# Unused products, earlier gate products and earlier table loads in the small modules of a four-layer network

## The chip, the core and the metric

The kernel runs on one core of a Trainium2 chip, as one launch. The engines of the core work side by side, each through its own queue of instructions: TensorE (PE) multiplies matrices and turns them, VectorE (DVE) and ScalarE (ACT) work on elements, GpSimd (POOL) fills and converts, and SyncE (SP) issues most of the DMAs. They meet only in semaphores. The metric is the device time of one execution in microseconds; lower is better.

## The reference

A state x of 128 rows by 256 channels goes through four layers. Each layer adds three things to x in turn, each computed from a normalised x: a cross-attention over 12544 context rows, a small attention among the 128 rows themselves, and a feed-forward part. Cut to its lines:

```
x = x + _L0_xattn_ref(_layernorm(x, axis=-1), ctx_1024, ...)
x = x + _L0_attn_ref(...)      # one head, softmax over columns
x = x + _L0_ffn_ref(...)       # 16 experts, tokens chosen by each expert
x = x + _L1_xattn_ref(...)
x = x + _L1_attn_ref(...)      # delta rule with convolutions and a fusion gate
x = x + _L1_ffn_ref(...)       # 8 experts, two per token, layernorm and Gelu
x = x + _L2_xattn_ref(...)
x = x + _L2_attn_ref(...)      # one head
x = x + _L2_ffn_ref(...)       # fixed-point Gelu
x = x + _L3_xattn_ref(...)
x = x + _L3_attn_ref(...)      # windowed, rotary
x = x + _L3_ffn_ref(...)       # 8 experts, the nearest centroid's gate
```

All is in float32. The layernorm needs 1/sqrt(var + eps); the attentions need an exponential; L1_ffn needs the exact Gelu; L3_ffn a sigmoid.

## The kernel before

The twelve parts are twelve modules, named L0x, L0a, L0f (cross-attention, attention, feed-forward), then L1x to L3f. Each is a block with one hand-written queue for each engine, and all engines meet at the end of each block, so the order is that of the code. The four cross-attentions take 400 to 600 us each and loop over the context; the change touches none of their loops. The other eight modules take 12 to 74 us each. They are chains: one engine hands 128 rows to the next, and most engines wait most of the time.

A module begins with a layernorm (`norm_vector`, L1370, on VectorE; `norm_scalar`, L1381, the square root on ScalarE): statistics, variance plus eps, root, reciprocal, and the normalised tile. TensorE then turns the tile (`turn_chunks`, L1388), VectorE copies the result from PSUM to SBUF, and projections follow (`project_rows`, `project_turned`).

`keep_busy(e, bank, ident, n)` (L1360, the product at L1363) issues n products of the identity with itself into a PSUM bank whose content nobody reads. It stands in TensorE's queue where it would otherwise wait, and before the wait. The profile shows each such product as two matmuls and two weight loads, so n = 10 reads x20. It holds what is queued behind it until it is through.

ScalarE holds one table of functions at a time. The compiler puts an ACT_TABLE_LOAD ahead of the first activation that needs another table. In the modules before, the load for the layernorm's root stands at the start of the module.

Places that the change and the prediction touch:

- L1a (`delta_rule_attention`): TensorE turns the k rows (L1992), waits for the v rows and turns them (L1996), runs 10 unused products, then turns the normalised k rows and the kb rows (L1391). At its end it runs 18 unused products, turns o, and multiplies by wo.
- L1f (`top_two_experts`): 8 first-layer products of 128 x 512 (L1753), each added to its bias and measured on VectorE; after the fourth, VectorE picks two experts per token and makes `weight`. After the eighth, TensorE turns `weight` (L1757), VectorE copies it, TensorE multiplies it by b2 (L1760), and VectorE starts `acc` with it (L1840); then come the roots' reciprocal (L1842), the normalising (L1844), the turns, Gelu on ScalarE (L1799) and the second layer.
- L2f (`rounded_ffn`): the output bias is a product of one row (L2443) behind the last of the second-layer products (L2441).
- L3a (`window_attention`) and L3f (`nearest_expert`): L3a ends with a turn and the product by wo. L3f normalises x twice, scores the centroids (L3f_p_g), makes the input of each expert (L2768, with g and b that ScalarE's queue has loaded), and runs two first layers (L1399) before the first second layer (L1407). The turn of `weight` (L2720) and its product with b2 (L2723) stand between, and VectorE waits for both ahead of its half of the hidden rows (L2805).

## Time and profile before

| | us |
|---|---|
| median of 3 runs | 2319.34 |
| lowest, highest | 2318.71, 2323.18 |
| profiled execution | 2316.36 |
| its span | 2314.5 |
| mean granted clock in the span | 0.993 |
| PE, DVE, ACT, POOL busy | 2215.0, 1624.2, 1476.6, 414.0 |
| L1a, from its first VectorE instruction to that of L1f | 73.8 (1123.9 to 1197.7) |
| L1f, to that of L2x | 52.3 (1197.7 to 1250.0) |
| L3a, to that of L3f | 26.5 (2213.7 to 2240.2) |
| L3f, to the issue of the output's DMA | 71.6 (2240.2 to 2311.8) |

The span is what the profiler saw of the program; the execution took 1.9 us more than it. TensorE counts as busy for 96% of the span, but that holds the unused products and the pipelined ends of matmuls. The granted clock is a share of 2.4 GHz: 1.00 is 2.4 GHz, 0.50 is 1.2 GHz, and a value between is a stretch with both.

### The profile page before, as it was taken

To read this page: it belongs to the slowest core of one execution; us is meant where nothing else is said; L and a number is where in the kernel's file an instruction comes from. 1 tells how busy PE (TensorE), PEld (TensorE's weight loads), DVE (VectorE), ACT (ScalarE), POOL (GpSimd) and SP (SyncE) were. 2 spreads that over 40 slices of the span, in tenths; PEclk is the share of its full clock that TensorE was granted. 3 is DMA by queue.
4 is the path that set the end of the run, shared out by engine and by line. 5 is a ranking of instruction groups with operands and counts; after the bars stand their busy time and mean duration, and the time that the engine had idled before them with its cause. 6 is when DMAs were issued, how large, how long until landed. Compare 5 with 4: busy or idle time off the path is not lost. (4 is left out here: it accounts for less than half of the span.)

```text
span 2314.5 us, 75395 instructions
## 1 busy us (share of the span) xinstructions
PE 2215.0 (96%) x30367; PEld 1924.6 (83%) x30367; DVE 1624.2 (70%) x3699; ACT 1476.6 (64%) x3173; POOL 414.0 (18%) x356
## 2 busy tenths in 40 slices
PE   8999999988999999999899999999998999999989
PEld 7888888887888888888678888888887888888878
DVE  6787777536777777777664778777735877877732
ACT  3766776635878788878543677676642766667621
POOL 3222121003121212120002222222002212222000
PEclk9999999999999999999999999999999999999999
DMA  7777777375444444433512777777616777777471
GB/s 149 127 126 129 130 131 116 51 236 151 112 117 115 112 118 109 124 102 77 192 44 70 141 122 125 123 126 128 98 53 130 133 132 130 119 126 128 67 263 58
DMA packets 152487, 280.07 MB, mean 121 GB/s; under 512 B 32829, under 2 KB 72078, under 8 KB 152218
## 3 DMA queue, kind: packets, MB, share of 16 engines
q1 hardware_dynamic: 148842, 272.18, 57.2%
q10 hardware_dynamic: 3376, 4.03, 0.6%
q8 instruction: 203, 3.33, 0.6%
q14 instruction: 66, 0.54, 0.1%
HBM read 120.94 MB, written 0.33 MB: 52 GB/s over the span
## 5 line engine op out<-in xcount | busy, mean ns | idle before, releaser
L580 DVE CUSTOM_DVE_ANT_0 L1x_p_s<-L1x_p_s,L1x_mask,L1x_neg_max 128x512 f32<-128x512 f32 (+1 forms) x400 | 288.6, 742 | 56.5 <-PE L1x_p_s L339 54.3
L1259 DVE TENSOR_REDUCE L0x_tops<-L0x_m_bank 128x1 f32<-128x448 f32 x448 | 262.7, 618 | 83.0 <-PE L0x_m_bank L993 80.7
L1259 DVE TENSOR_REDUCE L3x_tops<-L3x_m_bank 128x1 f32<-128x448 f32 x448 | 262.4, 618 | 83.2 <-PE L3x_m_bank L993 80.9
L1259 DVE TENSOR_REDUCE L2x_tops<-L2x_m_bank 128x1 f32<-128x448 f32 x448 | 262.7, 619 | 79.7 <-PE L2x_m_bank L993 77.5
L473 ACT ACTIVATE L1x_prob<-L1x_p_s,L1x_neg_max 128x512 f32<-128x512 f32 (+1 forms) x400 | 274.5, 686 | 68.7 <-DVE L1x_neg_max L580 66.6
L1157 ACT ACTIVATE L0x_prob<-L0x_s_bank 128x512 f32<-128x512 f32 x448 | 220.4, 549 | 88.7 <-PE L0x_s_bank L1006 82.8
L1157 ACT ACTIVATE L3x_prob<-L3x_s_bank 128x512 f32<-128x512 f32 x448 | 220.4, 549 | 87.6 <-PE L3x_s_bank L1006 81.7
L1157 ACT ACTIVATE L2x_prob<-L2x_s_bank 128x512 f32<-128x512 f32 x448 | 220.4, 549 | 87.4 <-PE L2x_s_bank L1006 81.5
L348 PE MATMUL L1x_p_t<-net_ident,L1x_prob 128*128 128x128 f32 x1568 | 239.5, 274 | 13.6 <-ACT L1x_probT L189 11.4
L348 PEld LDWEIGHTS L1x_p_t<-net_ident,L1x_prob 128*128 128x128 f32 x1568 | 191.9, 141 | 56.7 <-ACT L1x_probT L189 23.5
L339 PE MATMUL L1x_p_s<-L1x_k_stack,L1x_q_stack 96*128 96x512 f32 (+1 forms) x400 | 181.7, 456 | 2.2 <-DVE L1x_q_stack L563 1.9
L189 ACT COPY L1x_probT<-L1x_p_t 128x512 f32<-128x512 f32 (+1 forms) x300 | 172.3, 575 | 1.8 <-PE L1x_p_t L348 1.6
L1006 PEld LDWEIGHTS L0x_s_bank<-L0x_q_sub,L0x_k_stack 52*128 52x128 f32 x1568 | 117.8, 187 | 24.8 <-issue 17.3
L1006 PEld LDWEIGHTS L3x_s_bank<-L3x_q_sub,L3x_k_stack 52*128 52x128 f32 x1568 | 117.5, 186 | 25.0 <-issue 17.4
L1006 PEld LDWEIGHTS L2x_s_bank<-L2x_q_sub,L2x_k_stack 50*128 50x128 f32 x1568 | 117.4, 186 | 24.8 <-issue 17.3
L1006 PE MATMUL L0x_s_bank<-L0x_q_sub,L0x_k_stack 52*128 52x128 f32 x1568 | 122.2, 266 | 3.0 <-ACT L0x_prob L1157 3.0
L1006 PE MATMUL L3x_s_bank<-L3x_q_sub,L3x_k_stack 52*128 52x128 f32 x1568 | 122.0, 266 | 3.0 <-ACT L3x_prob L1157 3.0
L1006 PE MATMUL L2x_s_bank<-L2x_q_sub,L2x_k_stack 50*128 50x128 f32 x1568 | 121.9, 265 | 2.8 <-ACT L2x_prob L1157 2.8
L364 PE MATMUL L1x_p_oT<-L1x_probT,L1x_v 128*32 128x128 f32 x3136 | 106.4, 276 | 0.5 <-ACT L1x_probT L189 0.5
L269 POOL CAST L1x_ctx_part<-L1x_ctx 128x1024 fp32r<-128x1024 f32 x24 | 25.4, 1058 | 409.7 <-DMA L1x_ctx<-in_ctxT 213.6
L1026 PE MATMUL L0x_s_bank<-L0x_prob,L0x_v 128*32 128x128 f32 x3136 | 97.2, 274 | 0.3 <-ACT L0x_prob L1157 0.3
L1026 PE MATMUL L3x_s_bank<-L3x_prob,L3x_v 128*32 128x128 f32 x3136 | 97.2, 274 | 0.3 <-ACT L3x_prob L1157 0.3
(821 smaller groups left out, 5589.4 us busy)
## 6 DMA issues: line engine op xcount, KB each, us to landing
L0x_k_stack<-L0x_kT SPq DMA_DIRECT2D x333, 112.0 KB, 4.0
L2x_k_stack<-L2x_kT SPq DMA_DIRECT2D x333, 112.0 KB, 4.0
...
```

The lines of the kernel that those rows point to most:

```text
L189: copy(probT[:, h % PT_RING, 0:nk], p_t[h % T_RING][:, 0:nk]).then_inc(sem(copied(h)), 1)
L269: e.tensor_copy(high, ctx[:, odd, :, 0:nk]).then_inc(sem("ctx_high"), 1)
L339: e.matmul(p_s[h % S_RING][:, 0:nk], q_stack[0:ROWS, h, :], k_stack[0:ROWS, odd, h // 2, 0:nk], start=True, stop=True).then_inc(sem("score ...
L348: i = e.transpose(p_t[h % T_RING][:, t * P:(t + 1) * P], prob[:, h % P_RING, t * P:(t + 1) * P], ident[:])
L364: i = e.matmul(p_oT[VW * s:VW * s + VW, g * P:(g + 1) * P], v[:, odd, t, h, :], probT[:, h % PT_RING, t * P:(t + 1) * P], start=t == 0, st ...
L473: e.activation(prob[:, h % P_RING, 0:nk], p_s[h % S_RING][:, 0:nk], ACT.Exp, bias=neg_max[:, odd, h:h + 1], scale=-1.0).then_inc(sem("expe ...
L580: e.tensor_tensor_reduce(s, s, mask[:, odd, 0:nk], -1.0, neg_max[:, 1 - odd, h:h + 1], ALU.add, ALU.min, neg_max[:, odd, h:h + 1]).then_in ...
L1006: mm = e.matmul(s_bank[s_at(u, r) % RING][:, at * P:(at + 1) * P], k_stack[rows_of(r), b % 2, slot_of(u), t * P:(t + 1) * P], q_sub[rows_o ...
L1026: mm = e.matmul(bank[32 * n:32 * n + VW, 2 * P:3 * P], v[:, b % 2, t, n // 2 * 8 + 2 * j + n % 2, :], prob[:, (2 * q + t // 4) % 3, n, t % ...
L1157: e.activation(prob[:, k % 3, u % 2 * 2 + r, 0:nt, :].rearrange("p t n -> p (t n)"), s_bank[n % RING][:, 0:nt * P], ACT.Exp).then_inc(sem( ...
L1259: e.tensor_reduce(tops[:, b % 2, h, half:half + 1], m_bank[n % RING][:, 0:HALF], AX, ALU.max).then_inc(sem("m_free"), 1)
```

## The change

Four kinds of edit, in the modules outside the cross-attentions' loops. A function `next_root` is new: an activation of one column with Sqrt, whose result nobody reads, put at the end of ScalarE's queue in all modules but L1a, L1f and L3f; the table is then loaded there. In L1f a Gelu of one column stands behind the roots. Unused products are added or taken away at 23 places in L1a, L1f, L2f, L3a and L3f. In L1f and L3f the turn of `weight`, its copy and its product with b2 stand earlier, and in L2f the bias product comes first.

```diff
@@ cross_attention, cross_attention_turned, one_head_attention, token_choice_experts, rounded_ffn, window_attention: end of the scalar queue
+            next_root(e, st)
...
+def next_root(e, st):
+
+    e.activation(st["warm"][:], st["ident"][:, 0:1], ACT.Sqrt)
...
@@ top_two_experts, tensor
-            keep_busy(e, p_y[1], ident, 10)
+            keep_busy(e, p_y[1], ident, 8)
             e.wait_ge(sem("ln_normed"), 1)
             turn_chunks(e, ident, p_x, xn).then_inc(sem("xn_turned"), 1)
-            keep_busy(e, p_y[1], ident, 6)
+            keep_busy(e, p_y[1], ident, 4)
             e.wait_ge(sem("xnT_copied"), 1)
             e.wait_ge(sem("gate_loaded"), 16)
             project_rows(e, p_g[:, 0:E], xnT, gate).then_inc(sem("gated"), 1)
-            keep_busy(e, p_y[1], ident, 3)
...
                 i.then_inc(sem("h_made"), 1)
-            e.wait_ge(sem("small_weights"), 80)
-            e.wait_ge(sem("weighted"), 1)
-            e.transpose(p_x[0:E, 0:P], weight[:], ident[:]).then_inc(sem("weight_turned"), 1)
-            keep_busy(e, p_y[1], ident, 12)
+                if x_ == 5:
+                    e.wait_ge(sem("small_weights"), 80)
+                    e.wait_ge(sem("weighted"), 1)
+                    e.transpose(p_x[0:E, 0:P], weight[:], ident[:]).then_inc(sem("weight_turned"), 1)
             e.wait_ge(sem("weightT_copied"), 1)
             e.matmul(p_g[:, 0:D], weightT[:], b2[:], start=True, stop=True).then_inc(sem("b2_made"), 1)
-            keep_busy(e, p_y[1], ident, 7)
+            keep_busy(e, p_y[1], ident, 13)
...
                 if x_ == 1:
-                    keep_busy(e, p_y[1], ident, 9)
+                    keep_busy(e, p_y[1], ident, 5)
@@ scalar
             e.activation(rstd[:, 0, :], rstd[:, 1, :], ACT.Sqrt).then_inc(sem("h_roots"), 1)
+            e.activation(st["warm"][:], ident[:, 0:1], ACT.Gelu)
@@ vector
+                if x_ == 5:
+                    e.wait_ge(sem("weight_turned"), 1)
+                    e.tensor_copy(weightT[:], p_x[0:E, 0:P]).then_inc(sem("weightT_copied"), 1)
...
-            e.wait_ge(sem("weight_turned"), 1)
-            e.tensor_copy(weightT[:], p_x[0:E, 0:P]).then_inc(sem("weightT_copied"), 1)
-            e.wait_ge(sem("b2_made"), 1)
-            link(e.tensor_tensor(acc[:], xn[:], p_g[:, 0:D], ALU.add))
...
+                if x_ == 1:
+                    e.wait_ge(sem("b2_made"), 1)
+                    e.tensor_tensor(acc[:], xn[:], p_g[:, 0:D], ALU.add).then_inc(sem("acc_begun"), 1)
@@ delta_rule_attention, tensor
             t.then_inc(sem("k_turned"), 1)
+            keep_busy(e, bank[7], ident, 14)
             e.wait_ge(sem("v_activated"), 1)
...
-            keep_busy(e, bank[6], ident, 18)
+            keep_busy(e, bank[6], ident, 28)
             e.wait_ge(sem("o_done"), 1)
             turn_chunks(e, ident, bank[1], flat(o)).then_inc(sem("o_turned"), 1)
+            keep_busy(e, bank[6], ident, 2)
             e.wait_ge(sem("oT_copied"), 1)
             project_rows(e, bank[2][:, 0:D], oT, wo).then_inc(sem("out_made"), 1)
+            keep_busy(e, bank[6], ident, 3)
@@ rounded_ffn, tensor
-            keep_busy(e, p_x, ident, 24)
+            keep_busy(e, p_x, ident, 22)
             e.wait_ge(sem("w2_loaded"), 32)
+            e.wait_ge(sem("steps"), 1)
+            e.matmul(p_o[:, 0:D], steps[:], b2[:], start=True, stop=False)
...
-            e.matmul(p_o[:, 0:D], steps[:], b2[:], start=False, stop=True).then_inc(sem("out_made"), 1)
+            i.then_inc(sem("out_made"), 1)
@@ window_attention, tensor
-            keep_busy(e, p_o, ident, 30)
+            keep_busy(e, p_o, ident, 33)
             e.wait_ge(sem("affine"), 1)
...
-            keep_busy(e, p_o, ident, 4)
+            keep_busy(e, p_o, ident, 10)
             e.wait_ge(sem("rotated"), 1)
...
+            keep_busy(e, p_o, ident, 3)
             e.wait_ge(sem("qkT_copied"), 1)
...
+            keep_busy(e, p_o, ident, 3)
             e.wait_ge(sem("probT_copied"), 1)
...
+            keep_busy(e, p_x, ident, 2)
             e.wait_ge(sem("o_done"), 1)
             turn_chunks(e, ident, p_t, o[:].rearrange("p h d -> p (h d)")).then_inc(sem("o_turned"), 1)
+            keep_busy(e, p_x, ident, 2)
             e.wait_ge(sem("oT_copied"), 1)
             project_rows(e, p_v[:, 0:D], oT, wo).then_inc(sem("out_made"), 1)
+            keep_busy(e, p_x, ident, 3)
@@ nearest_expert, tensor
-            keep_busy(e, p_y[1], ident, 10)
+            keep_busy(e, p_y[1], ident, 8)
             e.wait_ge(sem("ln_normed"), 1)
             turn_chunks(e, ident, p_x, xn).then_inc(sem("xn_turned"), 1)
+            keep_busy(e, p_y[1], ident, 2)
...
             project_rows(e, p_g[:, 0:E], xnT, cent).then_inc(sem("aff_made"), 1)
+            keep_busy(e, p_y[1], ident, 4)
             e.wait_ge(sem("ln2_normed"), 1)
             turn_chunks(e, ident, p_x, xh).then_inc(sem("xh_turned"), 1)
 
-            keep_busy(e, p_y[1], ident, 10)
+            keep_busy(e, p_y[1], ident, 5)
...
+                if n == 0:
+                    e.wait_ge(sem("weighted"), 1)
+                    e.transpose(p_x[0:E, 0:P], weight[:], ident[:]).then_inc(sem("weight_turned"), 1)
                 if n == 1:
                     e.wait_ge(sem("bias_loaded"), 32)
-                    e.wait_ge(sem("weighted"), 1)
-                    e.transpose(p_x[0:E, 0:P], weight[:], ident[:]).then_inc(sem("weight_turned"), 1)
-                    keep_busy(e, p_y[1], ident, 4)
                     e.wait_ge(sem("weightT_copied"), 1)
@@ vector
             e.tensor_tensor(weight[:], one[:], alpha[:], ALU.mult).then_inc(sem("weighted"), 1)
+            link(e.tensor_tensor(x[:], x[:], xn[:], ALU.add))
             e.wait_ge(sem("weight_turned"), 1)
             e.tensor_copy(weightT[:], p_x[0:E, 0:P]).then_inc(sem("weightT_copied"), 1)
-            link(e.tensor_tensor(x[:], x[:], xn[:], ALU.add))
-            e.wait_ge(sem("b2_made"), 1)
-            link(e.tensor_tensor(x[:], x[:], p_g[:, 0:D], ALU.add))
...
+                if x_ == 1:
+                    e.wait_ge(sem("b2_made"), 1)
+                    link(e.tensor_tensor(x[:], x[:], p_g[:, 0:D], ALU.add))
```

TensorE's queue in L1f, from the first-layer products (L1f_w is the experts' weights, net_ident the identity, x12 how often) to the first turns of the hidden rows, before:

```order
L1753 MATMUL L1f_p_h<-L1f_w,L1f_xnT 128x512 x16
L1757 MATMUL L1f_p_x<-net_ident,L1f_weight 8x128
L1363 MATMUL L1f_p_y<-net_ident 128x128 x12
L1760 MATMUL L1f_p_g<-L1f_b,L1f_weightT 128x256
L1363 MATMUL L1f_p_y<-net_ident 128x128 x7
L1391 MATMUL L1f_p_t<-net_ident,L1f_h 128x128 x8
L1363 MATMUL L1f_p_y<-net_ident 128x128 x9
```

and in the changed kernel:

```order
L1761 MATMUL L1f_p_h<-L1f_w,L1f_xnT 128x512 x12
L1766 MATMUL L1f_p_x<-net_ident,L1f_weight 8x128
L1761 MATMUL L1f_p_h<-L1f_w,L1f_xnT 128x512 x4
L1768 MATMUL L1f_p_g<-L1f_b,L1f_weightT 128x256
L1365 MATMUL L1f_p_y<-net_ident 128x128 x13
L1398 MATMUL L1f_p_t<-net_ident,L1f_h 128x128 x8
L1365 MATMUL L1f_p_y<-net_ident 128x128 x5
```

The turn of `weight` has moved ahead of the last two experts, the 12 unused products between it and the bias product are gone, and 7 have become 13.

VectorE's queue in L3f, from `weight` to the first expert's output, before:

```order
L2793 TENSOR_TENSOR L3f_weight<-L3f_one,L3f_alpha 128x8
L2795 COPY L3f_weightT<-L3f_p_x 8x128
L2796 TENSOR_TENSOR net_x<-net_x,L3f_xn 128x256
L2798 TENSOR_TENSOR net_x<-net_x,L3f_p_g 128x256
L2805 TENSOR_SCALAR L3f_h<-L3f_p_h,L3f_b 128x128 x4
L2768 TENSOR_SCALAR L3f_xe<-L3f_xhT,L3f_g,L3f_b 128x128 x2
```

and in the changed kernel:

```order
L2818 TENSOR_TENSOR L3f_weight<-L3f_one,L3f_alpha 128x8
L2819 TENSOR_TENSOR net_x<-net_x,L3f_xn 128x256
L2821 COPY L3f_weightT<-L3f_p_x 8x128
L2828 TENSOR_SCALAR L3f_h<-L3f_p_h,L3f_b 128x128 x4
L2793 TENSOR_SCALAR L3f_xe<-L3f_xhT,L3f_g,L3f_b 128x128 x2
L2828 TENSOR_SCALAR L3f_h<-L3f_p_h,L3f_b 128x128 x4
L2793 TENSOR_SCALAR L3f_xe<-L3f_xhT,L3f_g,L3f_b 128x128 x2
L2835 TENSOR_TENSOR net_x<-net_x,L3f_p_g 128x256
```

The addition of the bias product (L3f_p_g) has moved behind the hidden rows of the first two experts.

ScalarE's queue around L0a, before (a branch is the seam between two modules):

```order
L761 UNCONDITIONAL_BRANCH
L1480 UNCONDITIONAL_BRANCH
L1385 ACT_TABLE_LOAD
L1385 ACTIVATE L0a_ln_rstd<-L0a_ln_rstd 128x1
L1487 ACTIVATE L0a_kT<-L0a_p_k,L0a_bk 128x128 x2
L1494 ACT_TABLE_LOAD
L1494 ACTIVATE L0a_prob,L0a_total<-L0a_s,L0a_low 128x128
L1440 UNCONDITIONAL_BRANCH
```

and in the changed kernel:

```order
L1370 ACT_TABLE_LOAD
L1370 ACTIVATE net_warm<-net_ident 128x1
L762 UNCONDITIONAL_BRANCH
L1487 UNCONDITIONAL_BRANCH
L1392 ACTIVATE L0a_ln_rstd<-L0a_ln_rstd 128x1
L1494 ACTIVATE L0a_kT<-L0a_p_k,L0a_bk 128x128 x2
L1501 ACT_TABLE_LOAD
L1501 ACTIVATE L0a_prob,L0a_total<-L0a_s,L0a_low 128x128
L1370 ACT_TABLE_LOAD
L1370 ACTIVATE net_warm<-net_ident 128x1
L1447 UNCONDITIONAL_BRANCH
```

The load stands ahead of the seam, and none stands ahead of the module's own root. The same holds at nine seams (into L0a, L0f, L1x, L1a, L2a, L2f, L3x, L3a and L3f).

## Rows read from the trace of the kernel before

**Rows 1.** Windows: length, busy us (count) of PE, PEld, DVE, ACT, POOL, clock, DMA, GB/s.
```profile
1134.00:1137.40 3.40, 0.01 (x1) 0.00 (x0) 3.04 (x11) 3.26 (x9) 0.00 (x0) 1.00 1.03 368
...
1195.90:1202.90 7.00, 6.24 (x28) 5.53 (x27) 1.86 (x7) 0.66 (x2) 0.60 (x16) 0.51 0.40 126
```

**Rows 2.** Timeline, the start of L0a and its end.
```profile
464.52 1.28 ACT L1385 ACT_TABLE_LOAD   x1 [3.91 <-PEq L761]
464.52 2.31 PEld L1363 LDWEIGHTS L0a_p_o<-net_ident 128*128 128x128 f32 x20 [0.46 <-issue]
...
465.23 0.15 DVE L1375 TENSOR_SCALAR L0a_ln_rstd<-L0a_ln_mean_var 128x1 f32<-128x1 f32 x1
...
466.75 0.25 PEld L1391 LDWEIGHTS L0a_p_x<-net_ident,L0a_xn 128*128 128x128 f32 x2
...
475.01 0.19 ACT L1494 ACTIVATION_READ_ACCUMULATOR L0a_prob<-L0a_s,L0a_low 128x1 f32 x1
...
476.50 0.42 DVE L1527 TENSOR_TENSOR net_x<-net_x,L0a_p_o 128x256 f32<-128x256 f32 x1 [0.79 <-PE L0a_p_o L1478]
```

**Rows 3.** Timeline, L1a, TensorE and VectorE; columns: start, duration, engine, line, operation.
```profile
1137.57 3.94 PEld L1363 LDWEIGHTS L1a_bank<-net_ident 128*128 128x128 f32 x20
...
1138.06 0.42 DVE L2239 TENSOR_TENSOR L1a_kb<-L1a_nat,L1a_beta 128x256 f32<-128x256 f32 x1
```

**Rows 4.** Timeline from the end of L1a into L1f.
```profile
1187.76 4.10 PEld L1363 LDWEIGHTS L1a_bank<-net_ident 128*128 128x128 f32 x36
...
1193.99 0.42 DVE L2360 TENSOR_TENSOR L1a_o<-L1a_o,L1a_onorm 128x256 f32<-128x256 f32 x1
...
1195.42 1.54 PE L1407 MATMUL L1a_bank<-L1a_wo,L1a_oT 128*128 128x256 f32 x4 [0.52 <-DVE L1a_oT L2362]
...
1197.69 4.34 PEld L1363 LDWEIGHTS L1f_p_y<-net_ident 128*128 128x128 f32 x20 [1.45 <-issue]
...
1199.02 0.41 DVE L1378 TENSOR_SCALAR L1f_xn<-net_x,L1f_ln_mean_var,L1f_ln_rstd 128x256 f32<-128x256 f32 x1
1201.91 0.44 PEld L1391 LDWEIGHTS L1f_p_x<-net_ident,L1f_xn 128*128 128x128 f32 x2
...
1205.04 0.30 PEld L1753 LDWEIGHTS L1f_p_h<-L1f_w,L1f_xnT 128*128 128x128 f32 x2
```

**Rows 5.** Timeline, the end of L3a and the first third of L3f.
```profile
2237.30 2.08 PE L1407 MATMUL L3a_p_v<-L3a_wo,L3a_oT 128*128 128x256 f32 x4 [0.52 <-DVE L3a_oT L2624]
...
2240.17 4.07 PEld L1363 LDWEIGHTS L3f_p_y<-net_ident 128*128 128x128 f32 x20 [1.52 <-issue]
...
2241.52 0.44 ACTq L2738 DMA_DIRECT2D L3f_b<-in_L_ffn_ln_b  x1
...
2246.95 3.94 PEld L1363 LDWEIGHTS L3f_p_y<-net_ident 128*128 128x128 f32 x20
...
2247.72 1.12 DVE L2768 TENSOR_SCALAR L3f_xe<-L3f_xhT,L3f_g,L3f_b 128x128 f32<-128x128 f32 x4
...
2250.82 7.23 PEld L1399 LDWEIGHTS L3f_p_h<-L3f_xe,L3f_w 128*128 128x128 f32 x64
...
2261.66 0.51 PEld L1407 LDWEIGHTS L3f_p_y<-L3f_w,L3f_h 128*128 128x128 f32 x3 [2.21 <-issue]
```

**Rows 6.** Timeline of L1f behind its last first-layer product.
```profile
1222.31 0.21 ACT L1792 ACTIVATE L1f_rstd<-L1f_rstd 128x8 f32<-128x8 f32 x1 [13.54 <-DVE L1f_rstd L1836]
...
1223.32 0.42 DVE L1840 TENSOR_TENSOR L1f_acc<-L1f_xn,L1f_p_g 128x256 f32<-128x256 f32 x1 [0.86 <-PE L1f_p_g L1760]
...
1224.77 0.91 PEld L1391 LDWEIGHTS L1f_p_t<-net_ident,L1f_h 128*128 128x128 f32 x8
...
1225.56 1.28 ACT L1799 ACT_TABLE_LOAD   x1 [3.04 <-PE L1f_p_t L1391]
```

**Rows 7.** Timeline, the end of L2f.
```profile
1746.02 0.69 PE L2443 MATMUL L2f_p_o<-L2f_b,L2f_steps 1*128 1x256 f32 x2
```

**Rows 8.** Tile L3f_b: time from issue to landing of its DMAs.
```profile
DMA to landing us min/median/max: 6.0/6.0/6.0
```

More of the change, by code:

```diff
@@ L1211, in _ @@
                     rise(g // WAVES - 1)
+            next_root(e, st)
         @block.vector
@@ L1494, in _ @@
             e.activation(prob[:], s[:], ACT.Exp, bias=low[:, 0:1], accum_out=total[:]).then_inc(sem("exped"), 1)
+            next_root(e, st)
         @block.vector
@@ L1637, in _ @@
                              bias=b12[:, 1, x_:x_ + 1]).then_inc(sem("h2_done"), 1)
+            next_root(e, st)
         @block.vector
@@ L1845, in _ @@
                                 ALU.subtract, ALU.mult).then_inc(sem("h_normed"), 1)
+                if x_ == 1:
+                    e.wait_ge(sem("b2_made"), 1)
+                    e.tensor_tensor(acc[:], xn[:], p_g[:, 0:D], ALU.add).then_inc(sem("acc_begun"), 1)
+            e.wait_ge(sem("acc_begun"), 1)
             for x_ in range(E):
@@ L2440, in _ @@
                 for fc in range(half * 4, half * 4 + 4):
-                    e.matmul(p_o[:, 0:D], hT[:, fc, :], w2[:, fc, :], start=fc == 0, stop=False)
-            e.wait_ge(sem("steps"), 1)
-            e.matmul(p_o[:, 0:D], steps[:], b2[:], start=False, stop=True).then_inc(sem("out_made"), 1)
+                    i = e.matmul(p_o[:, 0:D], hT[:, fc, :], w2[:, fc, :], start=False, stop=fc == FC - 1)
+            i.then_inc(sem("out_made"), 1)
         @block.scalar
@@ L2469, in _ @@
             ends(1)
+            next_root(e, st)
         @block.vector
@@ L2585, in _ @@
                              accum_out=total[:, h:h + 1]).then_inc(sem("exped"), 1)
+            next_root(e, st)
         @block.vector
@@ L2819, in build @@
     m = Module(nc, "net")
-    st = {n: m.sb(n, shape) for n, shape in (("x", [P, D]), ("ident", [P, P]), ("stack_rows", [P, 2]))}
+    st = {n: m.sb(n, shape) for n, shape in (("x", [P, D]), ("ident", [P, P]), ("stack_rows", [P, 2]), ("warm", [P, 1]))}
     with nc.Block() as block:
```

## The prediction

> **What bounds the kernel now.** The page first: TensorE is busy for 96% of the span, but in the eight small modules much of that is unused products, so the share says nothing there. The table under "Time and profile before" gives their lengths; L1a, L1f, L3a and L3f, in which nearly all edits lie, take 224 us together. What a change there is worth must be read link by link in the timeline.
>
> The windows view comes second, for the granted clock. TensorE stood still from 1134.0 to 1137.4, and ran the whole stretch from 1195.9 to 1202.9 at 0.51, which is the 1.2 GHz level for nearly all of it [rows 1]. The level is also seen in the unused products: 10 of them, x20 in a row, take 2.31 us in L0a [rows 2], but 3.94 in L1a [rows 3], 4.34 at the start of L1f [rows 4], 4.07 and 3.94 in L3f [rows 5]. Each slow stretch follows one in which TensorE did little.
>
> Third, the timeline around those products, for what stood behind them. In L1a the last input of the next turn is ready at 1138.48 (1138.06 + 0.42), and the unused products ahead of the turn run until 1141.51 [rows 3]. In L1f the normalised x is ready at 1199.43, and its turn starts at 1201.91 [rows 4]. So at half clock the unused products themselves are the path.
>
> **The change, term by term.** At full clock two passes of an unused product take 0.223 us of the queue: in L0a the turn starts 2.23 us after the first of 10 products [rows 2]. All terms are made against the profiled execution's own 2316.36 us.
>
> Term 1, the middle of L1a. The 14 new products fill 3.1 us of the 3.4 us in which TensorE waits for the v rows [rows 1]; they end before 1137.2 and cost nothing (at half clock they would cost 2.7 us). If the clock then stays up, the next 10 take 2.31 instead of 3.94 [rows 2, 3]: -1.6. The kb rows are ready a microsecond before that. Bounds: 0 if the clock falls anyway, -1.6.
>
> Term 2, the end of L1a. 28 products from 1187.76 take 28 x 0.223 = 6.2 us and end at 1194.0; o is ready at 1194.41 (1193.99 + 0.42), so they fit with 0.4 us to spare [rows 4]. The product by wo then takes about 1.04 us in place of 1.54 [rows 4]: the same product at half clock took 2.08 [rows 5], and full clock halves that. But three unused products now follow it, 0.67 us, against VectorE's last addition of 0.42 us beside them; the block ends with the later of them. I take 0.3 of the 0.5 as given back: -0.2 (bounds 0 and -0.5).
>
> Term 3, the head of L1f. Before, from 1197.69 to the first expert's product at 1205.04: 7.35 us [rows 4]. After: 8 products are through at +1.8, and x is normalised at +1.74 (1199.43 less 1197.69 [rows 4]), so the turn starts at +1.8. The copy of its result (0.42) and the steps around it end at about +2.9; 4 products behind the turn are through at +2.95. The gate product takes 0.45, and no unused products follow: the first expert's product starts at +3.45. That is -3.9. Bounds: -1.4 if the clock is low (8 x 0.434 = 3.5 in place of 4.3, 5 others fewer), -4.2. The expert biases come by DMA on ScalarE's queue at the same distance from the start as before, and could hold the first addition by up to a microsecond.
>
> Term 4, the tail of L1f. Before, the roots are done at 1222.52, but VectorE then waits for the bias product and adds it until 1223.74; only then come the reciprocal, the normalising, the turn at 1224.77, a table load of 1.28 from 1225.56 and the Gelu at 1226.84 [rows 6]. After: the reciprocal follows the roots at once, the turn starts at about 1223.35, and the Gelu table has been loaded since 1223.8; the 13 products end at 1222.9. Gelu starts at about 1224.15: -2.7. The copy of `weight` (0.27) and the addition to `acc` (0.42) now stand among other work of VectorE, which has over a microsecond of slack at both places. Bounds: -1.3 (the load alone) and -2.7.
>
> Term 5, the end of L2f: the bias product of 0.69 us at 1746.02 goes from the path [rows 7]: -0.6 (bounds -0.3 and -0.7).
>
> Term 6, L3a. It waits for weights at its head, so 33 products for 30 cost nothing; the others (0.45 to 1.3 us) fit into waits of TensorE. What remains is the product by wo, 2.08 us at half clock [rows 5]: 1.05 less, of which the trailing products give back 0.25: -0.8 (bounds 0 and -1.05).
>
> Term 7, L3f. Before, from 2240.17 to the first second layer at 2261.66: 21.5 us [rows 5]. Two waits would go: the unused products at half clock and the bias product ahead of VectorE's hidden rows. But a third is right behind them. The experts' g and b are loaded by ScalarE's queue; b was issued at 2241.52 and landed 6.0 us later, at 2247.5, and the experts' inputs were started at 2247.72 [rows 5, 8]: 7.4 us after the module's start, for b as for VectorE. The issue hangs on the variance and not on the table, so it stays at +1.35, and b lands at +7.35 though the rest is ready at about +4.9. Hence: inputs of the first expert at +8.0, two first layers of 7.23 together [rows 5] until +15.3, turn and bias product 0.6, second layer at +15.9. That is -5.6. Bounds: -3.0 if only the reordering counts, and -7.6 if b lands early.
>
> Term 8, the tables. A load of 1.28 us stands ahead of each root [rows 2], and in L0a the variance is ready at 465.38, 0.42 us before the load ends at 465.80 [rows 2]. Moving it makes x ready 0.4 us earlier at nine places. But the turn there starts at 466.75, exactly 2.23 us after the 10 unused products did [rows 2]: TensorE's own products hold it, whenever x is ready. They stay 10 or more in L0a, L0f, L1x, L1a, L2a, L2f, L3x and L3a, so nothing is gained; only L3f has 8, and is counted in term 7. The moved loads cost nothing where ScalarE has time: in L0a, the tightest, its last instruction ends at 475.20, load and root by 476.7, VectorE at 476.92 [rows 2]. Term: 0 (bounds +1 and -3.8, nine times 0.42).
>
> The Trainium skill ("ScalarE: Activation LUTs", What ACT_TABLE_LOAD costs) speaks against this: it adds a drain of about 1.38 us to each switch. By that rule load and root would end at 478.1 in L0a, 1.2 us behind VectorE, and the sum would be some 3 us smaller over the tight seams; the trace does not agree, since in L0a the loads before cost no more than their 1.28 us: the turn, which stands behind the root, three steps of VectorE and 1.28 us of load, started at 2.23 us, and with a drain it could not have.
>
> Sum: -1.6 -0.2 -3.9 -2.7 -0.6 -0.8 -5.6 = -15.4. 2316.36 - 15.4 = 2301.0 for a profiled execution; the median of the runs lies 3.0 above it, so the median after should be near 2303.9.
>
> **Rivals.** (a) The clock falls elsewhere or stays low at one of the four places, since new idle times lie differently. For it speaks that L3f still has TensorE waiting 1 to 2 us for b; against it, that the waits of TensorE between L0a's few rows went without one: its unused products took 2.31 us, full clock [rows 2]. It takes terms 1 to 3 (5.7) or much of 6 and 7 (about 4): about 2309. The Trainium skill ("TensorE: Matmul & The Clock Gate", Part 1) says that the activity window is free-running, so the same kernel counts different numbers of slow matmuls from run to run; if so, part of what the trace shows as lost is luck of that execution, and 2309 would be the time. One profile cannot show that.
>
> (b) The table loads do pay, because the products' hold on the turn is softer than it looks, or b lands earlier: up to 3.8 and 2.0 more; in the middle, some 5 us, about 2299.
>
> (c) Slower. The added products run at half clock and become the path: 0.434 us each. At 1187.76 they would end at 1199.9 in place of 1194.0, 5.5 us after o is ready; the 14 cost 2.7, and 33 in L3a 14.3 us, against 7.3 at full clock: some 7 us behind the weights. Terms 4, 5 and the reordering of L3f give back 6.3. Put together: 5.5 + 2.7 + 7 - 6.3 = 8.9, about 2328. It decides as soon as the 28 take more than 6.65 us, 0.238 us each. Against it: before, 18 in the same place took 4.10 us, full clock [rows 4].
>
> (d) The change doesn't do what it says: the compiler puts a load ahead of the roots again. The rows of ScalarE's queue show none, so for the tables this is out; it would cost 9 x 0.2 us and leave about 2306.
>
> **Chances.** Forecast 0.68, (a) 0.16, (b) 0.10, (c) 0.03, (d) 0.03. What this measurement can tell from no change is about 0.2%, 4.6 us. The forecast, (b) and (d) are all faster by more; of (a) and its worse mixtures I leave 0.04 within 4.6 us, and 0.02 to mixtures of (c). Faster 0.92, same 0.04, slower 0.04. Range: 2298 to 2310.
>
> **What would show it.** In the changed profile: clock 1.00 from 1134 through L1f's head and from L3a's end into L3f; x20 behind the v turn in 2.3 us; from L1f's start to its first expert's product 3.5 us; no table load between L1f's first hidden turns and Gelu; from L3f's start to the first second layer 15.9 us, with TensorE waiting for VectorE's L3f_xe; L0a, L0f and L2a as long as before. A module's end set by ScalarE's table load, or an x20 of over 3 us, would prove me wrong.

## The result and the profile after

| | before | after |
|---|---|---|
| median of the runs, us | 2319.34 (5 runs: the three above and two more) | 2303.03 (5 runs) |
| lowest, highest | 2316.30, 2323.18 | 2300.38, 2305.28 |
| profiled execution, us | 2316.36 | 2303.03 |
| its span, mean clock | 2314.5, 0.993 | 2301.2, 0.996 |

The changed kernel takes 0.9925 of the time of the kernel before (95% interval 0.9909 to 0.9940), 16.3 us less by the medians; 2303.9 was forecast. The profiled execution, however, was forecast at 2301.0 and took 2303.03: only the median came out, see below. The share of busy time tells nothing here either: TensorE is at 96% in both.

```profile
PE 2214.2 (96%) x30421; PEld 1923.9 (84%) x30421; DVE 1624.9 (71%) x3699; ACT 1479.2 (64%) x3183; POOL 412.9 (18%) x356
```

The lengths of the modules tell it. Each is the distance between two modules' first VectorE instructions (of L3f to the span's end, good to 0.05 us). The columns e1 and e9 are two further executions of the same changed kernel (e1 and e9 below).

| us | before | after | e1 | e9 | forecast change |
|---|---|---|---|---|---|
| L0x | 464.55 | 469.44 | 481.48 | 466.78 | 0 |
| L0a | 12.67 | 12.57 | 12.47 | 12.54 | 0 |
| L0f | 53.24 | 53.11 | 53.18 | 53.38 | 0 |
| L1x | 593.45 | 591.66 | 593.66 | 591.88 | 0 |
| L1a | 73.81 | 73.42 | 71.64 | 71.72 | -1.8 |
| L1f | 52.30 | 45.59 | 45.58 | 45.59 | -6.6 |
| L2x | 460.60 | 461.60 | 461.59 | 460.49 | 0 |
| L2a | 12.76 | 12.70 | 12.79 | 12.84 | 0 |
| L2f | 24.56 | 24.65 | 24.68 | 24.09 | -0.6 |
| L3x | 465.78 | 461.43 | 466.42 | 466.38 | 0 |
| L3a | 26.48 | 26.69 | 26.72 | 28.30 | -0.8 |
| L3f | 74.30 | 68.34 | 68.29 | 68.21 | -5.6 |

The small modules together went down by 13.05 us in the profiled execution. The cross-attentions, whose loops were not edited, moved by +4.9, -1.8, +1.0 and -4.35, which happens to add up to -0.25. One span against another would mislead: e1 is the same program, and its span is 2318.5.

The clock first, in the stretches that answer to [rows 1], and at the end of L1a (columns: length, busy of PE, PEld, DVE, ACT, POOL, clock, DMA, GB/s):

```profile
1136.90:1140.30 3.40, 3.31 (x30) 3.11 (x28) 3.08 (x10) 3.25 (x9) 0.00 (x0) 1.00 0.99 349
1189.20:1197.10 7.90, 7.90 (x58) 7.90 (x58) 5.19 (x17) 2.75 (x4) 0.00 (x0) 0.78 0.00 0
1198.50:1205.80 7.30, 7.00 (x46) 5.57 (x45) 2.85 (x11) 0.98 (x2) 0.59 (x16) 1.00 0.45 128
2232.80:2239.60 6.80, 5.60 (x46) 5.28 (x46) 3.43 (x12) 1.69 (x3) 0.60 (x16) 1.00 1.02 326
```

The first stretch is the one in which TensorE stood still before; now it is busy for 3.3 of the 3.4 us. The heads of L1f and L3f (third and fourth) run at 1.00, where before L1f's had 0.51 and L3f's was at half clock (1.2 GHz) for its first 3.7 us. But the second stretch is at 0.78: half clock has come up at a place that had full clock before. The timeline of L1a shows both (columns: start, duration, engine, line, operation):

```profile
1136.81 3.21 PEld L1365 LDWEIGHTS L1a_bank<-net_ident 128*128 128x128 f32 x28
...
1140.65 2.31 PEld L1365 LDWEIGHTS L1a_bank<-net_ident 128*128 128x128 f32 x20
```
and before, the v turn and the turn behind the 10 products:
```profile
1137.40 0.20 PEld L1996 LDWEIGHTS L1a_bank<-net_ident,L1a_act 128*128 128x128 f32 x2 [3.63 <-DVE L1a_act L2233]
...
1141.43 0.25 PEld L1391 LDWEIGHTS L1a_bank<-net_ident,L1a_nat 128*128 128x128 f32 x2
```
The end of L1a and the head of L1f, after:
```profile
1189.22 7.96 PEld L1365 LDWEIGHTS L1a_bank<-net_ident 128*128 128x128 f32 x56
...
1195.45 0.43 DVE L2375 TENSOR_TENSOR L1a_o<-L1a_o,L1a_onorm 128x256 f32<-128x256 f32 x1
1197.10 0.25 PEld L1398 LDWEIGHTS L1a_bank<-net_ident,L1a_o 128*128 128x128 f32 x2
...
1200.17 1.86 PEld L1365 LDWEIGHTS L1f_p_y<-net_ident 128*128 128x128 f32 x16 [0.46 <-issue]
...
1201.97 0.24 PEld L1398 LDWEIGHTS L1f_p_x<-net_ident,L1f_xn 128*128 128x128 f32 x2
...
1203.51 0.30 PEld L1761 LDWEIGHTS L1f_p_h<-L1f_w,L1f_xnT 128*128 128x128 f32 x2
```

The 14 new products take 3.21 us ahead of the v turn, and the 10 behind it 2.31 in place of 3.94 [rows 3]; from the v turn to the next turn it is 2.40 us (1140.48 to 1142.88) in place of 4.03. At the end of L1a, 28 products take 7.96 us in place of the 6.2 expected. o is ready at 1195.88 (1195.45 + 0.43), and the turn starts at 1197.10: TensorE's own products hold it for 1.2 us. Then L1f: its first expert's product comes 3.34 us after the start, 7.35 before [rows 4].

The tail of L1f, to lay beside [rows 6]:

```profile
1220.78 0.21 ACT L1800 ACTIVATE L1f_rstd<-L1f_rstd 128x8 f32<-128x8 f32 x1 [11.16 <-DVE L1f_rstd L1848]
1221.01 1.28 ACT L1801 ACT_TABLE_LOAD   x1
...
1221.86 0.87 PEld L1398 LDWEIGHTS L1f_p_t<-net_ident,L1f_h 128*128 128x128 f32 x8
...
1222.62 1.51 ACT L1808 ACTIVATE L1f_a<-L1f_p_t,L1f_b1n,L1f_g 128x128 f32<-128x128 f32 x4
```

From the roots to Gelu it takes 1.84 us (1220.78 to 1222.62), before 4.54 (1222.31 to 1226.85). The table load starts behind the root and lies beside VectorE's first normalised rows and the turn; ScalarE starts Gelu 0.33 us behind it.

L3f, to lay beside [rows 5]:

```profile
2232.83 1.86 PEld L1365 LDWEIGHTS L3f_p_y<-net_ident 128*128 128x128 f32 x16 [0.46 <-issue]
...
2234.18 0.44 ACTq L2763 DMA_DIRECT2D L3f_b<-in_L_ffn_ln_b  x1
...
2238.25 0.42 DVE L2787 COPY L3f_xhT<-L3f_p_x 128x256 f32<-128x256 f32 x1 [1.07 <-PE L3f_p_x L1398]
...
2239.64 1.11 DVE L2793 TENSOR_SCALAR L3f_xe<-L3f_xhT,L3f_g,L3f_b 128x128 f32<-128x128 f32 x4 [0.97 <-DMA L3f_b<-in_L_ffn_ln_b]
...
2247.81 0.69 PE L2748 MATMUL L3f_p_g<-L3f_b,L3f_weightT 8*128 8x256 f32 x2
...
2248.43 0.73 PEld L1414 LDWEIGHTS L3f_p_y<-L3f_w,L3f_h 128*128 128x128 f32 x4 [0.33 <-issue]
```

VectorE stands still for 0.97 us until b has landed, and starts the experts' inputs 6.8 us after the module's start; the second layer follows at +15.6 in place of 21.5. And the seams, in L0a and L2f:

```profile
470.31 0.20 ACT L1392 ACTIVATE L0a_ln_rstd<-L0a_ln_rstd 128x1 f32<-128x1 f32 x1 [3.30 <-DVE L0a_ln_rstd L1382]
...
471.64 0.25 PEld L1398 LDWEIGHTS L0a_p_x<-net_ident,L0a_xn 128*128 128x128 f32 x2
...
475.11 1.13 PE L1406 MATMUL L0a_p_q<-L0a_xnT,L0a_wq 128*128 128x128 f32 x8 [1.64 <-DMA L0a_bv<-in_L_attn_bv]
...
480.00 1.28 ACT L1370 ACT_TABLE_LOAD   x1
...
481.29 0.42 DVE L1535 TENSOR_TENSOR net_x<-net_x,L0a_p_o 128x256 f32<-128x256 f32 x1 [0.79 <-PE L0a_p_o L1485]
```
```profile
1725.26 3.81 PE L2447 MATMUL L2f_p_h<-L2f_xnT,L2f_w 128*128 128x128 f32 x32 [1.37 <-DMA L2f_w<-in_L_ffn_w]
```

In L0a the root starts with no load before it, 0.87 us after the module's start in place of 1.26. The turn still comes at +2.23, and behind it the q product waits for bv's DMA until +5.7. The load at the end (480.00 to 481.28) lies under VectorE's last steps.

### The profile page after: what moved, and what is told of

It is laid out like the page before. It is cut to its first block and busy times, and to the rows that moved or that the text cites. A ratio compares the mean times of both kernels' runs of the same rounds, so it can differ in the third digit from the quotient of the medians.

```text
span 2301.2 us, 75514 instructions
## 1 busy us (share of the span) xinstructions
PE 2214.2 (96%) x30421; PEld 1923.9 (84%) x30421; DVE 1624.9 (71%) x3699; ACT 1479.2 (64%) x3183; POOL 412.9 (18%) x356
## 3 DMA queue, kind: packets, MB, share of 16 engines
q10 hardware_dynamic: 3376, 4.03, 0.6%
## 6 DMA issues: line engine op xcount, KB each, us to landing
L3f_w<-in_L_ffn_w SPq DMA_DIRECT2D x16, 1024.0 KB, 12.1
```

## The experiments

All were profiled, so that each module is compared with its own length in the tables. The timed ratios stand beside them, each with its 95% interval, against the kernel before on the same chip: e1 to e4 on one chip, e5 to e8 on a second, e9 to e11 on a third.

**e1 and e9: the changed kernel again, twice.** No edit.

> The changed kernel, unaltered, in another execution. Theory 1 (the gain lies in L1f and L3f and is fixed by the code): L1f is 45.6 us again and L3f 68.3, each within 0.2; L0x, which read 469.4 in the first profile and 464.6 in that of the kernel before though its loop was not edited, lies anywhere between 463 and 471, as do L3x (461 to 467) and L2x. Whether TensorE falls to half clock behind the fusion gate of L1a (28 products in 7.96 us) is luck of the execution: L1a is 73.4 with it and 72.2 without. Rival (the longer L0x belongs to the change, by the table load at its end or by code that lies elsewhere): L0x is 469 to 470 again, and L1a 73.4 again.

> The changed kernel once more, beside the version with all three further edits, on one chip. Theory 1: L1f 45.6 and L3f 68.3 within 0.2 for the third time; L1a 71.6 if TensorE keeps the clock behind the fusion gate, 73 to 75 if not; no half clock at the heads of L1f and L3f nor at L1a's v turn. Ratio to the kernel before 0.993. Rival (the places of half clock are free): it shows at one of these three places.

Measured: in e1 0.9932 of the kernel before (0.9913 to 0.9951), in e9 0.9934 (0.9905 to 0.9963). L1f is 45.58 and 45.59, L3f 68.29 and 68.21. L0x reads 481.5 and 466.8: its length belongs to the execution, not to the change, and 481.5 is well outside the range that I had given. L1a is 71.64 and 71.72, without half clock:

```profile
1202.68 6.33 PEld L1365 LDWEIGHTS L1a_bank<-net_ident 128*128 128x128 f32 x56
...
1209.38 0.20 PEld L1398 LDWEIGHTS L1a_bank<-net_ident,L1a_o 128*128 128x128 f32 x2 [0.37 <-DVE L1a_o L2375]
```

The 28 products take 6.33 us there and the turn waits for o (0.37 us idle) and not for them. The expected 72.2 was too high by 0.6; 0.35 of it is the head, where the v turn came 13.14 us after the start, 13.49 before. L3a in e9 took 28.30: TensorE was at half clock from 2215.8 to 2219.2.

**e2: the table edits alone**, on the kernel before.

```diff
+            next_root(e, st)                                   (nine scalar queues)
+            e.activation(st["warm"][:], ident[:, 0:1], ACT.Gelu)   (L1f)
```

> The kernel before with only the ten table edits: the root's table loaded at nine seams, and Gelu's behind the roots of L1f. Theory 1 (TensorE's 10 unused products and the weights' DMAs hold each head, not the root): L0a, L0f, L1a, L2a, L2f and L3a as long as before within 0.15 us, save for the landing of their weights; L1f shorter by 1.3 (Gelu's load), L3f by 0 to 0.1; in all -1.3, ratio 0.9994. Rival (the root is on the path at each seam): 0.4 less in each of nine modules, in all -5.1, ratio 0.9978.

Measured: 0.9989 (0.9970 to 1.0008). L0a, L0f and L2a are within 0.11 us of before. The interval holds both the 0.9994 of theory 1 and the 0.9978 of the rival; the lengths decide between them. L1a, L2f and L3a, which I had expected within 0.15 as well, are 0.73, 0.23 and 0.34 shorter; in L1a and L3a 0.40 and 0.42 of it lie from the product by wo to the end, where half clock stood before. L1f is 49.10, 3.2 less. From the roots to Gelu it takes 3.26 us, before 4.54: 1.28 less. But the second layer follows Gelu after 2.08 us (1221.21 to 1223.29), before after 1.56 (1226.85 to 1228.41), because the 9 unused products in between now hold it; in the changed kernel they are 5, and it is 1.55. The second layer in the kernel before:

```profile
1228.41 1.59 PEld L1407 LDWEIGHTS L1f_p_y<-L1f_w,L1f_a 128*128 128x128 f32 x8 [0.68 <-ACT L1f_a L1799]
```

The head is 2.45 less, and that is clock, without any edit that could steer it:

```profile
1195.78 2.31 PEld L1365 LDWEIGHTS L1f_p_y<-net_ident 128*128 128x128 f32 x20 [1.13 <-issue]
...
1200.68 0.30 PEld L1762 LDWEIGHTS L1f_p_h<-L1f_w,L1f_xnT 128*128 128x128 f32 x2
```
```profile
1217.95 0.21 ACT L1801 ACTIVATE L1f_rstd<-L1f_rstd 128x8 f32<-128x8 f32 x1 [12.83 <-DVE L1f_rstd L1846]
...
1221.21 1.15 ACT L1809 ACTIVATE L1f_a<-L1f_p_t,L1f_b1n,L1f_g 128x128 f32<-128x128 f32 x3 [1.54 <-PE L1f_p_t L1398]
...
1223.29 0.74 PEld L1414 LDWEIGHTS L1f_p_y<-L1f_w,L1f_a 128*128 128x128 f32 x4
```

The same 10 products, 4.34 us before, take 2.31 here, and the head takes 4.90 us with all its 19 products. So of the 4.0 us that L1f's head gained in the changed kernel, 2.45 (7.35 to 4.90) are clock and 1.56 (4.90 to 3.34) are fewer products. One small module went the other way: L3f took 76.4, with half clock in its head and again at its first second layer.

**e3: the moved instructions alone**, on the kernel before: the turn of `weight`, its copy and its product with b2 in L1f and L3f, and L2f's bias product first.

> The kernel before with only the moved instructions: in L1f and L3f the turn of weight, its copy and its product with b2, with the 12, 7 and 4 unused products beside them made 13 and 0, and in L2f the bias product first. Theory 1 (terms are separate waits): L1f -1.4 of its 52.3, L2f -0.6 (its weights' landing aside), L3f -3.0 of its 74.3, in all about -5, ratio 0.9978. Rival (the order is worth nothing while TensorE is at half clock around it, or it is worth all of the gain): L1f and L3f unchanged within 0.3, or L3f -6.

Measured: 0.9970 (0.9953 to 0.9986). L1f's tail from the roots to Gelu is 3.11 us, 1.43 less; its head was slower by 0.3, so L1f is 51.19 (-1.1, where -1.4 was expected). L2f is 0.45 shorter. L1a, which has no edit here, took 74.95, with 6.8 us of half clock around its v turn. L3f is 70.51, 3.8 less where 3.0 was expected: in this execution the 10 products behind the second turn ran at full clock (2.31 us for 3.94 before).

```profile
2246.34 2.31 PEld L1363 LDWEIGHTS L3f_p_y<-net_ident 128*128 128x128 f32 x20
...
2256.65 0.51 PEld L1407 LDWEIGHTS L3f_p_y<-L3f_w,L3f_h 128*128 128x128 f32 x3 [0.33 <-issue]
```

**e4: the numbers of unused products alone**, on the kernel before, at every place that the moves do not touch.

> The kernel before with only the numbers of unused products changed, at every place of the change that the moves do not touch. Theory 1: the clock is up in L1a's middle and at the heads of L1f and L3f, so L1f -3.9 (48.4), L3f -2.6 (71.7, b's landing holds the rest), L1a -0.4 to -1.8, L3a -0.8 from its first turn to its end; in all about -8, ratio 0.9965. Rival (the clock is luck, and the products do not steer it): half clock shows again at one of the heads of L1f and L3f in this execution, and its module gains less than 2.

Measured: 0.9983 (0.9966 to 1.0000), less than the 0.9965 expected. L1a is 71.94 (-1.9) and L1f 48.29 (-4.0). In L3f the first second layer starts at +18.7 in place of 21.5 (-2.8), as forecast; but TensorE fell to half clock just there, and L3f in all gained only 1.1:

```profile
2267.29 5.00 PEld L1407 LDWEIGHTS L3f_p_y<-L3f_w,L3f_h 128*128 128x128 f32 x16 [2.21 <-issue]
```

The 16 weight loads take 5.00 us; in the changed kernel's trace they take 3.32. Neither theory had half clock at that place. What stands ahead of it is the wait of 2.2 us that e3's moves take away. Of the four traces that have this wait, three show half clock right there (e2, e4 and e11, not before); of the nine without it, none. So the moves save more than their own wait.

The three parts took 0.0011, 0.0030 and 0.0017 off the time, 0.0058 together, where the whole took 0.0068 in e1 on the same chip. That agrees within the intervals, which are 0.002 to each side; the timed runs alone could not price the parts more finely.

**e11: the 14 products alone**, on the kernel before.

```diff
             t.then_inc(sem("k_turned"), 1)
+            keep_busy(e, bank[7], ident, 14)
             e.wait_ge(sem("v_activated"), 1)
```

> The kernel before with only the 14 unused products ahead of the v turn in L1a. Theory 1 (TensorE's wait of 3.6 us there makes the clock fall): no half clock at the 10 products behind the v turn, which take 2.3 us in place of 3.9; the heads of L1f and L3f, with nothing changed before them, show half clock again at one of them at least. L1a about 72.2, L1f 50 to 52.5. Rival (the clock at L1a's turn is luck): x20 behind the v turn takes 3 to 4 us in this execution too.

```profile
1137.60 0.20 PEld L1997 LDWEIGHTS L1a_bank<-net_ident,L1a_act 128*128 128x128 f32 x2 [0.46 <-DVE L1a_act L2234]
...
1137.77 2.31 PEld L1363 LDWEIGHTS L1a_bank<-net_ident 128*128 128x128 f32 x20
...
1140.00 0.25 PEld L1391 LDWEIGHTS L1a_bank<-net_ident,L1a_nat 128*128 128x128 f32 x2
```
The heads of L3f and L1f, in the columns of the clock table above:
```profile
2244.00:2257.30 13.30, 12.11 (x56) 11.64 (x57) 5.54 (x23) 3.18 (x5) 0.60 (x16) 0.51 0.92 308
1195.00:1200.00 5.00, 4.24 (x25) 4.14 (x25) 1.76 (x6) 0.20 (x1) 0.59 (x16) 0.66 0.37 121
```

Measured, one execution: 2.31 us behind the v turn, 2.40 from that turn to the next, before 4.03. That is the 1.63 expected. L1a is 71.46, 2.35 less, but the other 0.72 lies elsewhere: the v turn came 0.32 earlier in the module, and from the product by wo to the end it took 1.89 us in place of 2.29, at full clock where the trace of before has half. The heads that were left as before have half clock again: 0.66 in L1f's, and in L3f a whole stretch of 13.3 us at 0.51, which makes L3f 77.62.

**e5: 8 products for 10 at five heads**, on the changed kernel.

```diff
-            keep_busy(e, ..., ident, 10)
+            keep_busy(e, ..., ident, 8)
             e.wait_ge(sem("ln_normed"), 1)
```

> The changed kernel with 8 unused products in place of 10 ahead of the first turn of L0a, L0f, L1a, L2a and L2f, so that the earlier root can start the turn at +1.8 us in place of +2.23. Theory 1 (behind the turn the head waits for DMAs: bv in L0a, the biases in L0f, the mask in L2a, w1 in L2f, Wv in L1a): the first turn moves by 0.45 at each, and the modules keep their lengths within 0.15 us, L1a at most 0.4 shorter; ratio to the changed kernel 1.000. Rival (the two products hid the gain of the table loads): each of the five is 0.4 shorter, 2.1 in all.

```profile
465.79 1.86 PEld L1365 LDWEIGHTS L0a_p_o<-net_ident 128*128 128x128 f32 x16 [0.46 <-issue]
...
471.54 0.63 PEld L1406 LDWEIGHTS L0a_p_q<-L0a_xnT,L0a_wq 128*128 128x128 f32 x5 [2.34 <-issue]
```

Measured: 0.9961 (0.9938 to 0.9983). The turn comes at +1.79, and the q product at +5.75 as ever, for bv. L0a is 12.67, L0f 53.32, L2a 12.94, L2f 24.31 (12.57, 53.11, 12.70 and 24.65 before this edit). So the two products hid nothing. L1a, expected at most 0.4 shorter, rose to 76.59: Wv's DMA made TensorE wait 1.33 us at its head, half clock followed, and at its end it was at half clock for 6.8 us, where the 28 products took 8.98. e8 and e10 have the same 8 products at that head, and L1a at 72.29 and 71.78, so the 76.59 belong to this execution.

**e6: L3f's small loads early**, on the changed kernel.

```diff
@@ window_attention, scalar
             norm_scalar(e, m, "ln2", scratch2)
+            load_small(e)            (the DMAs of L3f's cent, g and b)
@@ nearest_expert
-            e.dma_start(cent[:], chunked(w["cent"])).then_inc(sem("cent_loaded"), 16)
-            e.dma_start(g[:], w["g"]).then_inc(sem("affine_loaded"), 16)
-            e.dma_start(b[:], w["b"]).then_inc(sem("affine_loaded"), 16)
```

> The changed kernel with the DMAs of L3f's cent, g and b issued by ScalarE's queue in L3a, behind its two roots, in place of in L3f. Theory 1 (b's landing at +6.8 holds the experts' inputs, and cent's the second turn): the inputs start at +5.3 to +5.9 from the module's start in place of +6.78, L3f is 0.9 to 1.5 us shorter than 68.3, and VectorE no longer waits for L3f_b. Rival (the weights of the first expert or TensorE's products are right behind): L3f within 0.3 of 68.3.

```profile
2237.98 0.42 DVE L2791 COPY L3f_xhT<-L3f_p_x 128x256 f32<-128x256 f32 x1 [0.53 <-PE L3f_p_x L1398]
2238.44 1.11 DVE L2797 TENSOR_SCALAR L3f_xe<-L3f_xhT,L3f_g,L3f_b 128x128 f32<-128x128 f32 x4
```

Measured: 0.9960 (0.9933 to 0.9988). The experts' inputs start at +5.3 (2238.44 less 2233.13) and directly behind the copy; L3f is 66.87, 1.4 less. b's landing was the bound, as the third wait of term 7 says: 0.97 us. The rest is cent, which had held the gate product for 0.87 us; without it the copy ahead of the inputs starts at +4.85 in place of +5.39. The timed ratios of e5 and e6 (0.996 both) lie above the 0.993 that the changed kernel had on two other chips. On this chip it was not timed, so what these two edits do to the whole time is not shown; the lengths show what they do to their modules.

**e7: a semaphore for each group of weights** in L0a, L2a and L3a, and 22 unused products for 28 at the end of L1a, on the changed kernel.

```diff
-            e.wait_ge(sem("weights"), 16 * len(loads))
+            e.wait_ge(sem("wq_loaded"), 16)
             project_turned(e, p_q, wq, xnT)
+            e.wait_ge(sem("wk_loaded"), 16)
@@ window_attention, vector (and so on for wqkv, cos and sin, mask, wo)
-            e.wait_ge(sem("weights"), 16 * len(loads))
+            e.wait_ge(sem("ln_loaded"), 32)
@@ delta_rule_attention, tensor
-            keep_busy(e, bank[6], ident, 28)
+            keep_busy(e, bank[6], ident, 22)
```

> The changed kernel with one semaphore for each group of weights in L0a, L2a and L3a in place of one for all, so that each product waits for its own weights, in the order of their use (8 and 4 unused products at the head of L0a and L2a, 18 for 33 in L3a), and 22 unused products for 28 at the end of L1a. Theory 1 (the last of the small DMAs holds these heads): the query product starts at about +3.5 in place of +5.6 in L0a and +5.0 in L2a; L0a 11.0 (from 12.6), L2a 11.5 (12.7), L3a 24 (26.7), and L1a 71.6 whether or not TensorE is at half clock behind the fusion gate. Rival (DMAs of one queue land together, so a semaphore of one's own brings nothing, or idle TensorE falls to half clock): these three within 0.4 of before, or shorter heads with half clock in the rows behind.

```profile
1184.76 6.62 PEld L1365 LDWEIGHTS L1a_bank<-net_ident 128*128 128x128 f32 x44
...
1191.46 0.20 PEld L1398 LDWEIGHTS L1a_bank<-net_ident,L1a_o 128*128 128x128 f32 x2
```
```profile
2226.88 0.42 SPq L2719 DMA_DIRECT2D L3f_cent<-in_L_ffn_centroids  x1
...
2234.82 0.99 PE L1414 MATMUL L3f_p_g<-L3f_cent,L3f_xnT 128*128 128x8 f32 x4 [5.19 <-DMA L3f_cent<-in_L_ffn_centroids]
```

Measured: 0.9941 (0.9916 to 0.9967). L0a is 10.58, L2a 10.67, L3a 22.70, 2 to 4 us less each. In L1a TensorE was at half clock behind the fusion gate for 3.4 us; the 22 products ended at 1191.38, o was ready at 1191.41 and the turn started at 1191.46: 72.01, not 73.4. But L3f rose to 74.16. L3a is 4 us shorter, the DMAs of the experts' weights issued in it are not, and cent, issued behind them on SyncE's queue, landed 7.8 us after its issue. The last weights issued ahead of it had landed at +7.59, and cent at +7.75; in the changed kernel these are +3.26 and +3.42, in the kernel before +3.41 and +3.57. TensorE stood still for 5 us, and half clock followed (the 4 products behind the gate product took 1.83 us, where the same row in the changed kernel has 0.97). That was in neither theory.

**e8 and e10: all three edits together**, on the changed kernel.

> The edits of the last three together, on the changed kernel. Theory 1: the three terms add up, some 6 us less than the changed kernel: about 0.9905 of the kernel before. Rival (what is saved at a head is lost to half clock or to the experts' weights behind it): not below 0.992.

> The version with all three further edits once more. Theory 1: L0a 10.3, L3a 23.0, L3f 67.0 within 0.3 each, and 6 us less than the changed kernel on the same chip: ratio to the kernel before about 0.990. Rival (its last measurement was a lucky one): the ratio is that of the changed kernel within 0.001.

Two rows of e10:

```profile
466.93 0.23 PEld L1398 LDWEIGHTS L0a_p_x<-net_ident,L0a_xn 128*128 128x128 f32 x2
...
468.04 0.97 PEld L1406 LDWEIGHTS L0a_p_q<-L0a_xnT,L0a_wq 128*128 128x128 f32 x8
```
```profile
2232.07 1.11 DVE L2810 TENSOR_SCALAR L3f_xe<-L3f_xhT,L3f_g,L3f_b 128x128 f32<-128x128 f32 x4
```

Measured: e8 0.9918 (0.9885 to 0.9951); e10 0.9881 (0.9853 to 0.9909). e8 alone cannot tell its theory (0.9905) from its rival (not below 0.992); e10 can. It ran on the chip on which the changed kernel had 0.9934 (e9): medians of 2295.60, 2307.53 and 2322.41 us. L0a is 10.26 and 10.37, L3a 22.96 and 22.46, L3f 66.96 and 66.95: with cent loaded early, the shorter L3a costs L3f nothing. L2a is 10.77 in e10 but 12.38 in e8, where its own first weight landed late (TensorE waits 1.6 us for wq). This version beats both kernels: the changed kernel by 7.7 us in e8 and 9.7 in e10 by the lengths of L0a, L2a, L3a and L3f, and by 11.9 in e10 by the medians on one chip; about 6 was expected.

## Why the prediction was right, term by term

The sum was -15.4 and the medians say -16.3; on the chips of e1 and e9 they say -16.3 and -14.9. That the forecast number came out so closely is in part luck. The profiled execution is only 13.3 us shorter, 2.1 less than the sum: 1.2 by the clock at L1a's end, 0.7 and 1.0 by weights that landed later at the heads of L2f and L3a, less some 0.8 of small gains elsewhere. The forecast then put the median 3.0 above the profiled execution, as it had been before, and this time it was 0.0 above. The two misses nearly cancel. The mechanisms stand on the terms:

- Term 1 (L1a's middle, -1.6): as forecast. From the v turn to the next turn 4.03 us became 2.40, -1.63, in the changed kernel and in e11, which has this edit alone. No half clock was seen behind the v turn in any of the ten traces that have the 14 products, and it was in all three that lack them (before, e2, e3).
- Term 2 (L1a's end, -0.2): wrong in the profiled execution: the turn of o starts 1.23 us behind o, before 0.05. The product by wo and what follows it give back 0.2, as forecast (2.29 us became 2.09). The step that failed is "28 x 0.223 = 6.2 us": it takes full clock there for granted, because the 18 products had it in the one trace of before. What stands ahead is unchanged, yet half clock shows there in the first trace of the changed kernel, e2, e5, e6, e7 and e8, and not in before, e1, e3, e4, e9, e10 and e11. This was rival (c)'s mechanism, at one place and at 7.96 us against the 12.1 (28 x 0.434) that it had counted. Its sign, 28 products over 6.65 us, was given; its price of 5.5 us was not, since only 3.4 us there were at half clock, and its other two places, the 14 and the 33, stayed at full clock. In e1 and e9 the term is as forecast.
- Term 3 (L1f's head, -3.9): measured -4.0. The reason needs an addition: e2 had full clock there without the edit. So 1.56 us (seven products fewer) are certain, and 2.45 are gained only over executions like that of before. The bound of -1.4 for a low clock does not follow from the prediction's own prices: seven products fewer at 0.434 us are 3.0.
- Term 4 (L1f's tail, -2.7): measured -2.70; from e3 1.43 for the order, from e2 1.28 for Gelu's load. The prediction counted up to Gelu only; e2 shows that 0.5 of the load's share would have been lost behind it without the cut from 9 unused products to 5.
- Term 5 (L2f, -0.6): from the second layers' start to the end, 10.14 us became 9.57, -0.57; e3 has L2f 0.45 shorter. In the profiled execution the module's length hides it (24.65), since its w1 landed 1.6 us later at the head.
- Term 6 (L3a, -0.8): from the first turn on, 18.83 us became 18.02. The head again hides it: the mask's DMA took 4.8 us in place of 3.8.

```profile
DMA to landing us min/median/max: 3.8/3.8/3.8
```
```profile
DMA to landing us min/median/max: 4.8/4.8/4.8
```

- Term 7 (L3f, -5.6): measured -5.9 (the second layer at +15.6 for +21.5), with b landed at +6.7, not +7.35 (5.4 us from its issue, 6.0 before). e3 and e4 give 3.8 and 2.8 to the second layer's start, e6 shows that b was next.
- Term 8 (tables, 0): right. Nine loads moved, and no module but L1f and L3f is shorter for it. But the named reason was only the first of two: the unused products hold the turn, and e5 shows that without them a DMA does. The drain that the Trainium skill ("ScalarE: Activation LUTs", What ACT_TABLE_LOAD costs) adds to each switch is not in these traces: in L1f the load began at 1221.01, took 1.28 us, and the next activation started at 1222.30. In this trace 19 of the 31 loads have the next activation 0.01 us behind them.

Whether the clock is steered or luck can be counted over all 13 traces:

| half clock | with the waits of before | with the change's products or order |
|---|---|---|
| behind L1a's v turn | 3 of 3 | 0 of 10 |
| at L1f's head | 3 of 4 | 0 of 9 |
| from L3a's end into L3f's head | 4 of 4 | 0 of 9 |
| at L3f's first second layer | 3 of 4 | 0 of 9 |
| behind L1a's fusion gate (nothing ahead of it changed) | 1 of 4 | 5 of 9 |

So filling or removing a wait of TensorE does keep the clock up at the place behind it. Behind the fusion gate, where nothing was done, it comes and goes with the execution; 1 of 4 and 5 of 9 are too few to say that the change plays no part there. (In e5 and e7 half clock also showed in L3f at +6.3 and +6.7, behind a longer wait for cent.)

Of the rivals, (a) is partly true without having decided: half clock did come up elsewhere. The page of the Trainium skill ("TensorE: Matmul & The Clock Gate", Part 1) by which the same kernel counts slow matmuls differently from run to run is borne out: the three traces of the changed kernel have half clock at different places, L1a's end in one of three. (b) and (d) fell: e5 found nothing hidden, of b's 2.0 us only 0.6 came, and no load stands ahead of a moved root. I had put (a) at 2309; in effect it cost the profiled execution 1.2 us at L1a's end (of the 1.8 between 73.42 and e1's 71.64, the other 0.6 is the head, where the v turn came at +13.70 for +13.14), and the cross-attentions' -0.25 cost nothing.

What stays open: why L0x took 481 us in e1 and L3x 476 in e4. L0x had 17.1 us at half clock in e1 and 3.4 in before, L3x 13.6 in e4 and 3.4 in before. Some 10 to 14 us more at half speed lose 5 to 7 at most, of the 17 and 10.5 that these modules were longer; the rest has no explanation here, and no experiment went into it.
